# Attention and routed experts on one core: rotary tables kept in device memory, first x tile alone, last output by head pair, new order

## The reference

```python
q = _layernorm(q, q_norm_w, q_norm_b); k = _layernorm(k, k_norm_w, k_norm_b)
q = _rope(q, cos, sin); k = _rope(k, cos, sin)
scores = jnp.einsum('bhqd,bhkd->bhqk', q, k) / math.sqrt(D)
attn = jax.nn.softmax(jnp.where(causal[None, None], scores, -jnp.inf), axis=-1)
out = jnp.einsum('bhqk,bhkd->bhqd', attn, v)
out = out * jax.nn.sigmoid(gate)
return out @ w_o.T
```

## Time and profile before

| | |
|---|---|
| median of 3 runs | 1562.0 us (1560.15 to 1563.43) |
| profiled execution | 1561.02 us |
| its span, from first to last instruction | 1559.2 us |
| TensorE busy | 1508.5 us, 97% |
| TensorE weight loads busy | 1380.0 us, 89% |
| VectorE busy | 1310.9 us, 84% |
| ScalarE busy | 1154.7 us, 74% |
| GpSimd busy | 523.9 us, 34% |
| moved by DMA | 56.65 MB, 36 GB/s in the mean |

### The profile page before, as it was taken

The page is one execution under the profiler, slowest core; times in us unless marked ns, Lnnn a source line. Parts: engine busy times, 40 slices in busy tenths (PEclk is TensorE's granted clock), DMA queues, the critical chain, the costliest instruction groups (busy, mean ns, idle before and its releaser), DMA issues.

```text
span 1559.2 us, 29914 instructions
## 1 busy us (share of the span) xinstructions
PE 1508.5 (97%) x10589; PEld 1380.0 (89%) x10589; DVE 1310.9 (84%) x3011; ACT 1154.7 (74%) x3013; POOL 523.9 (34%) x726
## 2 busy tenths in 40 slices
PE   4999999999899999999999999999999999999998
PEld 3788999999899999999898999999998998899998
DVE  7999888787898888788789888887779988888875
ACT  3777777777778787787778777777777776776775
POOL 5544434320553222121046331221105535343200
PEclk9999999999999999999999999999999999999999
DMA  4400010001111000101211000110111101102000
GB/s 139 142 5 21 21 42 23 21 28 50 45 33 30 32 30 29 32 26 39 66 45 40 25 25 11 47 31 30 28 46 45 33 13 31 30 20 66 16 8 8
DMA packets 46646, 56.65 MB, mean 36 GB/s; under 512 B 4576, under 2 KB 43232, under 8 KB 46304
## 3 DMA queue, kind: packets, MB, share of 16 engines
q1 hardware_dynamic: 43424, 46.34, 9.5%
q0 software_dynamic: 3072, 8.39, 1.7%
HBM read 42.40 MB, written 18.35 MB: 39 GB/s over the span
## 4 chain that ended last, share of the span: by engine, by line
PE 74%; DVE 17%; ACT 5%; issue 2%; POOL 1%; DMA 1%; SPq 0%; DVEq 0%; ACTq 0%; POOLq 0%
PE bank L1286 39%; PE o_bank L1286 19%; PE pt_bank L1361 12%; DVE pT_lo L1219 3%; DVE neg_chunk_max L1205 2%; DVE t_same L1169 2%; DVE bank L1202 2%; PE bank L1339 1%; PE bank L1382 1%; DVE t_same L1165 1%; ACT probs L920 1%; DVE sumsq L1137 1%; DVE t_same L1153 1%; ACT gate L930 1%; ACT pT_hi L939 1%
## 5 line engine op out<-in xcount | busy, mean ns | idle before, releaser
L920 ACT ACTIVATE probs<-bank,neg_max 128x512 f32<-128x512 f32 (+3 forms) x640 | 399.8, 634 | 91.7 <-DVE neg_max L1212 57.6
L1219 DVE TENSOR_TENSOR pT_lo<-pt_bank,pT_hi 128x512 fp32r<-128x512 f32 (+1 forms) x576 | 368.7, 654 | 100.7 <-ACT pT_hi L939 96.8
L939 ACT ACTIVATE pT_hi<-pt_bank 128x512 fp32r<-128x512 f32 (+1 forms) x576 | 325.8, 578 | 131.3 <-PE pt_bank L1361 81.6
L1286 PE MATMUL o_bank<-pT_hi,v_hi 128*128 128x256 f32 x1088 | 333.7, 307 | 2.9 <-DVE pT_lo L1219 1.9
L1361 PE MATMUL pt_bank<-ident_f,probs 128*128 128x128 f32 x2176 | 315.2, 273 | 10.5 <-DVE pT_lo L1219 10.0
L785 POOL TENSOR_TENSOR t_swap<-qk_raw,table_swap 128x256 f32<-128x256 f32 (+1 forms) x256 | 135.4, 560 | 561.9 <-ACT t_same L889 560.9
L1286 PE MATMUL o_bank<-pT_hi,v_lo 128*128 128x256 f32 x1088 | 307.3, 282 | 0.0
L1286 PE MATMUL o_bank<-pT_lo,v_hi 128*128 128x256 f32 x1088 | 306.5, 282 | 0.0
L1205 DVE TENSOR_REDUCE neg_chunk_max<-bank 128x1 f32<-128x512 f32 (+1 forms) x384 | 244.8, 650 | 49.2 <-PE bank L1286 48.1
L1361 PEld LDWEIGHTS pt_bank<-ident_f,probs 128*128 128x128 f32 x2176 | 252.2, 140 | 36.0 <-DVE pT_lo L1219 13.5
L1286 PE MATMUL bank<-kT_hi,qT_hi 128*128 128x512 f32 (+3 forms) x640 | 244.0, 381 | 2.7 <-ACT probs L920 2.3
(11 more groups left out here) (163 smaller groups left out, 2974.6 us busy)
## 6 DMA issues: line engine op xcount, KB each, us to landing
rows<-xs SPq DMA_DIRECT2D x23, 256.0 KB, 2.7
expert_raw<-in_w_fc SPq DMA_DIRECT2D x23, 256.0 KB, 3.0
expert_raw<-in_w_proj SPq DMA_DIRECT2D x23, 256.0 KB, 2.7
yb<-rows SPq DMA_DIRECT2D x23, 256.0 KB, 2.1
xs<-in_x SPq DMA_DIRECT2D x11, 512.0 KB, 4.9
w_raw<-in_w_in SPq DMA_DIRECT2D x7, 640.0 KB, 4.3
angles<-in_cos_sin SPq DMA_DIRECT2D x64, 64.0 KB, 1.9
acc<-in_x SPq DMA_DIRECT2D x4, 512.0 KB, 8.3
```

Of the source, the lines that this page charges most:

```text
L920: act.activation(probs[:, u, h % 2, first:first + width], bank("scores", g, t, h, c)[:, 0:width], ACT.Exp, bias=neg_max[:, u, h % 2:h % 2 ...
L939: act.activation(pT_hi[:, n % PT_RING, 0:width], pt_bank[n % 2][:, 0:width], ACT.Copy)\
L1219: dve.tensor_tensor(pT_lo[:, n % PT_RING, 0:width], pt_bank[n % 2][:, 0:width], pT_hi[:, n % PT_RING, 0:width].bitcast(F32), ALU.subtract) ...
L1286: ins = pe.matmul(out_ap, s, m, start=(start and done == 1), stop=(stop and done == last))
```

## The change

Tables: `tables` stays in group 0 alone. Each set is stored to a new tensor in device memory (`table_store`, 384 KB), and the next `tables` waits until the store has landed. In groups 1 to 3 a load (`table_load`) brings a set back, into the same buffer for odd tiles and into the norm weights' buffer, no longer needed, for even ones. A load waits for all stores and for the rotation of the tile two before. The 48 angle loads of these groups go.

First x tile: the parts of x are 1, 3, 4, 4 and 4 tiles. Tile 0 is turned into one bank in one step.

Last output: for the last tile (3, 15), `og`, `og_hi` and `og_lo` are done by head pair, 256 columns each, and `OUT` is two steps of 6 matmuls into one bank.

Order: all of `BEGIN` and `DUE` are new, `BEGIN` is followed by three shifts for each tile, one for the products and the rotation, one for scores, one for gate and output; some of the planner's costs are new.

```diff
+X_PARTS = ((0, 1), (1, 4), (4, 8), (8, 12), (12, 16))
...
+def shift(g, t, k):
+
+    return BEGIN[2 * G * T + 1 + 3 * (g * T + t) + k]
...
-    for q in range(4):
-        add("sp", ("x_load", q), 0.5, [], 0, 512)
-        if q == 0:
+    for n, (first, last) in enumerate(X_PARTS):
+        add("sp", ("x_load", n), 0.5, [], 0, 128 * (last - first))
+        if n == 0:
...
-        if q == 1:
+        if n == 1:
             add("sp", ("ln_load",), 2.0, [], 0, 260)
...
+            b1, b2 = begin[g, t, 1] + shift(g, t, 2), begin[g, t + 1, 0] + shift(g, t, 2)
+            b0 = begin[g, t, 0] + shift(g, t, 0)
...
+            if g == 0:
+                if t >= 2:
+                    add("sp angles", ("angle_load", g, t), 0.45, [old(t2, "tables")], b0 + DUE["rope"] - 15, 64)
+                table = ("tables", g, t)
+                add("pool rope", table, 4.0, [old(t1, "rope_b"), old(t1, "same"), ("angle_load", g, t), ("ln_tables",),
+                                              ("table_store", t - 1) if t else None], b0 + DUE["rope"])
+                add("sp tables", ("table_store", t), 0.45, [table], 0, 384)
+            else:
+                table = ("table_load", g, t)
+                free = [("tables", 0, T - 1)] if (g, t) == (1, 0) else [old(t2 if n_t != T + 1 else t1, "rope_b")]
+                add("sp tables", table, 0.45, free + [("table_store", T - 1)], b0 + DUE["rope"] - DUE["table"], 384)
...
+            if (g, t) == LAST_TILE:
+                add("pe GT", ("GT", g, t), 0.44, [("gate_scale", g, t), ("o_take", g, t, 0), old(t1, "OUT")],
+                    b2 + DUE["turn_gate"])
+                for p in range(HG // 2):
+                    add("dve out", ("og", g, t, p), 0.33, [("GT", g, t), ("o_take", g, t, p)], b2 + DUE["og"])
+                    add("act og", ("og_hi", g, t, p), 0.3, [("og", g, t, p), old(t1, "OUT")], b2 + DUE["og"])
+                    add("dve og", ("og_lo", g, t, p), 0.33, [("og_hi", g, t, p)], b2 + DUE["og"])
+                add("pe OUT", ("OUT", g, t), 0.72, [("og_lo", g, t, 0), ("wo_lo", g)], b2 + DUE["out"])
+                add("pe OUT", ("OUT_rest",), 0.72, [("og_lo", g, t, 1)], b2 + DUE["out"])
...
+        def rotary(g, t):
+
+            return made_tables if g == 0 or t % 2 else norm_rows
...
+                elif kind == "table_store":
+                    w.wait_ge(tables_done, a[0] + 1)
+                    sp.dma_start(kept_tables[a[0]], made_tables[:]).then_inc(tables_kept, 16)
+                elif kind == "table_load":
+                    g, t = a
+                    n = g * T + t
+                    w.wait_ge(tables_kept, 16 * T)
+
+                    w.wait_ge(tables_done, T)
+                    if n > T:
+
+                        w.wait_ge(rotated_done, n - 1 if n > T + 1 else T)
+                    sp.dma_start(rotary(g, t)[:, 0:3], kept_tables[t]).then_inc(tables_back[t % 2], 16)
...
+                    w.wait_ge(tables_kept, 16 * n)
                     pool.tensor_tensor(halves(table_same[:]), halves(ln_w[:]), cos_t, ALU.mult)
```

More of the change, by code:

```diff
@@ L83, with part_of, turns_of @@
 HANDOVER = {"pe": (0.0, 0.2), "act": (0.28, 0.15), "dve": (0.2, 0.13), "pool": (0.3, 0.16), "sp": (0.2, 0.2)}
-BEGIN = [26.59, 41.38, 29.62, 36.09, 25.65, 50.81, 47.59, 46.92, 64.18, 72.49, 75.23, 89.37, 102.35, 116.24,
[10 rows of a table removed]
[L97 to L102, removed]
+BEGIN = [4.36, 34.3, 51.86, 41.22, 11.3, 27.98, 42.94, 18.5, 56.43, 89.16, 53.77, 79.19, 82.53, 79.26, 113.82,
[22 rows of a table added]
+DUE = {"table": 42.61, "qkv": -42.78, "rope": -12.87, "turn": -307.03, "v_lo": -73.08, "gate": 9.23,
+       "inv": -16.77, "turn_gate": 3.72, "og": 0.09, "out": 10.38, "out_add": 9.58, "scores": -12.51,
+       "max": -8.54, "exp": 27.94, "prob_step": 1.95, "pv": 9.95, "p_hi": -197.39, "p_lo": -1.87, "moe": 348.87,
+       "moe_step": 36.02, "moe_evict": 118.28, "moe_wait_1": 1.57, "moe_wait_2": -3.06, "route": 180.59,
+       "x0": 16.05, "x1": 4.78, "x2": -252.76, "x3": 50.02, "logits": -1.54, "gate_w": -221.0,
+       "scatter": -72.41, "next_w": -70.2, "wo": 702.79, "comb": 135.72, "window": 0.02}
+def part_of(t):
+    return min(n for n, (first, last) in enumerate(X_PARTS) if t < last)
+def turns_of(n):
+    return [(2 * n - 1 + c, c) for c in range(CT)] if n else [(0, None)]
 def chunks_of(t):
@@ L174, in program_steps @@
     add("pool ln", ("ln_tables",), 3.4, [("ln_load",)], 0)
[L175 to L188, removed]
+    when = [0.0, DUE["x0"], DUE["x1"], DUE["x2"], DUE["x3"]]
+    for n, (first, last) in enumerate(X_PARTS):
+        tiles, at = last - first, when[n]
+        add("dve stats", ("stats", n), 0.44 * tiles, [("x_load", n)], at)
+        add("pool x", ("x_rstd", n), 1.4, [("stats", n), ("pool_consts",)], at - 5)
+        add("dve norm", ("norm", n), 0.35 * tiles, [("x_rstd", n)], at)
+        for i, c in turns_of(n):
+            width = tiles * P if c is not None else CT * P
+            add("pe XT", ("XT", i), 0.11 * width / P if n else 0.55, [("norm", n), ("ident_load",)], at + 2)
+            add("act XT", ("xT_hi", i), 0.07 + width / 1200, [("XT", i)], at + 2)
+            add("dve XT", ("xT_lo", i), 0.07 + width / 960, [("xT_hi", i)], at + 2)
+        if n:
+            q = n - 1
+            add("pe L", ("L", q), 1.4, [("xT_lo", 2 * n), ("wr_lo",)], at + DUE["logits"])
+            add("act L", ("logit_copy", q), 0.48, [("L", q), ("LT", q - 1) if q else None], at + DUE["logits"])
+            add("pe L", ("LT", q), 0.25, [("logit_copy", q)], at + DUE["logits"] + 1)
+            add("dve logit", ("route", q), 0.2, [("LT", q)], at + DUE["logits"] + 1)
     for k in range(4, ROUTE_STEPS):
@@ L1010, in _ @@
                 elif kind == "stats":
[L1011 to L1013 removed]
+                    first, last = X_PARTS[a[0]]
+                    w.wait_ge(x_in[a[0]], 16)
+                    for t in range(first, last):
                         dve.bn_stats(x_stats[:, t, :], acc[:, t, :]).then_inc(stats_done, 1)
[L1015 removed]
+                    for t in range(first, last):
                         w.wait_ge(stats_done, t + 1)
@@ L1018, in _ @@
                 elif kind == "norm":
-                    q = a[0]
-                    w.wait_ge(rstd_x_done, 2 * q + 2)
-                    w.wait_ge(means_done, 4 * q + 4)
-                    for t in range(4 * q, 4 * q + 4):
+                    first, last = X_PARTS[a[0]]
+                    w.wait_ge(rstd_x_done, 2 * a[0] + 2)
+                    w.wait_ge(means_done, last)
+                    for t in range(first, last):
                         dve.tensor_scalar(xn[:, t, :], acc[:, t, :], x_mv[:, t, 0:1], x_rstd[:, t:t + 1],
```

158 lines of the change are left out of this document (88 added, 70 removed), and 32 rows, old and new, of the table BEGIN.

## The result

The changed kernel took 1569.8 us (median of 5, 1568.8 to 1571.3), the kernel before beside it 1562.0 (1560.2 to 1563.6). The ratio is 1.0049, interval 1.0034 to 1.0064: slower by 8 us, where 12 faster was forecast. The profiled execution took 1570.0 us, with a span of 1568.2. (Of the four executions behind the 1544.2 one took 3814 us; the other three took 1543.4 to 1544.7, with a median of 1543.7.)

The account below looks back on a forecast made before the run. TensorE was taken as the bound, busy 1508.5 us in a span of 1559.2. Sum: 1561.0 - 3.5 - 0.5 - 4 - 2 - 2 = 1549.0, 1550.0 beside the median; own range 1545 to 1554, whole range 1538 to 1566.

Parts of the forecast that it names:

- The new order: Whole kernel, new begin and due times: 2 us won, ends 11 won and 11 lost.
- not needed by any limit of an engine: Rival: the order does much better, partly from TensorE's 6.7 us idle between 1190 and 1350; 1540 us, chance 0.14.
- signs of being wrong: TensorE losing over 22.3 us from 60 to 1541 us, or VectorE's idle time before 25 us staying over 8.
- Rotary tables: Heads of groups 1 to 3: loaded tables let swaps start early; 3.5 us won, plus 0.5 from VectorE.
- VectorE crossed by GpSimd: Over 1100 us, less GpSimd table work speeds VectorE instructions by perhaps 2 to 6 us; 0.5 us won, ends 0 and 3.
- First x tile: Start of the kernel: a separate first tile wins VectorE idle time before 25 us; 4 us, ends 0 and 9.3.
- the term's first part: Start: norm weights stand behind 512 KB less, 2.9 us at 183 GB/s, of which half was taken.
- Last output: Tail: narrower gate instructions and six of twelve matmuls moved ahead; 2 us won, ends 1.3 and 2.6.
- The stores of the tables: Group 0: a store takes 3.5 us, held by 8.5 us before the next tables; priced at nothing.
- Rival (4): Slower: table loads stand behind waiting instructions on SyncE, 24 us, 1574; chance 0.16 shared with a worse order.
- an order that is worse by 5 or more: Whole kernel: the new order loses 5 us or more; chance 0.16 shared with late table loads on SyncE.

Follow-up runs that it names:

- late chips: Chips of the result and the first, second and fifth sets, where the kernel before took 1560.8 to 1562.0 us; on the others it took 1556.2 or 1556.3.
- r1: The changed kernel itself, unedited, run again on a chip where the kernel before took 1556.2 us: 1544.2 us, ratio 0.9918.
- fourth set: Set of three runs on another chip, the changed kernel unedited among them; the kernel before took 1556.2 us, the changed kernel 1544.2.
- r5: The kernel before with its 32 gathers replaced by GpSimd memsets, where the kernel before took 1560.8 us: 1556.7 us, 0.9973 of before.
- e1: The changed kernel with its 32 gathers replaced by GpSimd memsets of the same rows, same waits and order: 1544.6 us, 0.9893 of the kernel before.
- e10: The kernel before with its 32 gathers replaced by GpSimd memsets, where the kernel before took 1556.3 us: 1555.4 us, 0.9994 of before.
- short rows: The changed kernel gathering rows of 128 bytes instead of 1024: 1544.4 and 1545.2 us on two chips, 1569.1 where the kernel before took 1560.8.
- e4: The changed kernel with 32 more indirect DMAs, scatters into an unused tensor, in four runs of eight: 1585.4 us.
- e2: The changed kernel with its 32 gathers as plain GpSimd loads of the same size at the same places: 1544.9 us.
- e6: The changed kernel with each gather waiting until the one before it in its run of eight has landed: 1608.7 us.
- r6: The changed kernel with a wait ahead of every second gather, two in flight, where the kernel before took 1560.8 us: 1574.6 us.

## Why the prediction was wrong

**The step that failed is "The new order".** It took 2 us won, ends 11 won and 11 lost, and gave as its only reason for a loss that the planner's clock is not the chip's. It has no term for the gathers, so it put their cost at nothing. On the late chips the order lost 21 us on the gathers alone: they cost the changed kernel 25.2 (1569.8 - 1544.6, on two chips) and the kernel before 4.1 (1560.8 - 1556.7, on one chip). The prediction read the due times as a matter of VectorE, never asked where the new order puts the last expert slot, and so never saw that the 32 gathers, begun over 180 us before (1284.6 to 1464.7), would be pressed into 98 (1446.7 to 1544.2). The trace of before had the warning, TensorE's longest wait from 1284 to 1340 us, at 1296.5, behind its run of eight gathers:

```profile
PE pt_bank L1361 <- DVE pT_lo L1219: 2.1, 1, 2.1
```

It lies inside the stretch from 1190 to 1350, whose 6.7 us of idle time I called "not needed by any limit of an engine" and counted as something to win. The loss of 26.3 us of span against r1 is 18.3 of idle time (57.9 against 39.6) and 8.0 more of busy time, as the clock fell after each of the four large gaps (0.97 and 0.88 in the last two stretches, 1.00 in r1).

Both of the prediction's own signs of being wrong came: from 60 to 1541 TensorE loses 27.1 us, over 22.3, and VectorE is idle for 9.1 before 25, over 8. In r1 the first is gone (18.6) and the second is not (8.9).

**Without late updates the sum came out, in part by luck.** 1562.0 to 1550.0 was forecast, 12 us; measured are 12.0 on the fourth set's chip (12.5 by the median of 1543.7), and 12.1 on late chips between the two kernels without gathers (1556.7, 1544.6). The forecast has nearly all of it as idle time of TensorE. Between the traces of these two, r5 and e1, TensorE idles 6.4 us less (47.0, 40.6) and is busy 5.3 us less (1507.6, 1502.3). Most of these 5.3 stand in no term of the forecast, and the start gave less than half of its term. By parts:

- Rotary tables, 3.5 + 0.5 forecast. From 400 to 460 TensorE idles 1.8 us in place of 4.1, and its waits for the rotation fell from 2.7 to 1.2. From 800 to 860 and from 1200 to 1260, in the heads of groups 2 and 3, it idles 0.8 and 0.0 in place of 1.3 and 1.7. That makes 4.5, with what the order did there. The clock of 400 to 460, which the prediction counted too, went from 0.97 to 1.00, but it is 1.00 also in e10 and r5, the kernel before without gathers, so the tables have no part in it. The size is about right, the reason in part wrong. The swaps do start early, but the cycle did not shorten: rotations at 406.76 and 418.15, 11.4 us apart, as before. VectorE, busy 54.4 of the 60 us from 400 to 460, most likely sets the cycle. GpSimd and VectorE of the kernel after, head of group 1:

```profile
402.36 1.99 POOL L874 TENSOR_TENSOR t_swap<-qk_raw,made_tables 128x256 f32<-128x256 f32 x4 [6.32 <-ACT t_same L977]
...
406.76 1.40 DVE L1257 SCALAR_TENSOR_TENSOR t_same<-t_same,rstd,made_tables 128x128 f32<-128x128 f32 x5
...
412.77 1.99 POOL L874 TENSOR_TENSOR t_swap<-qk_raw,norm_rows 128x256 f32<-128x256 f32 x4 [7.15 <-ACT t_same L977]
...
418.15 1.40 DVE L1257 SCALAR_TENSOR_TENSOR t_same<-t_same,rstd,norm_rows 128x128 f32<-128x128 f32 x5
```

- VectorE crossed by GpSimd: the subtraction fell from 768 ns to 689, in the mean of all its tiles, and VectorE's busy time by 6.4 us, while GpSimd's share of the span fell from 34% to 22%. What TensorE had of it can't be read by itself. The row from the kernel after's groups by shape:

```profile
L1328 DVE TENSOR_TENSOR ogT_lo<-oT,ogT_hi 128x512 fp32r<-128x512 f32 x63 | 43.4, 689 | 0.8 <-ACT ogT_hi L1046 0.6
```

- First x tile, 4 forecast: TensorE idles 21.0 us before 60 in place of 22.8, so 1.8. The low half of tile 0's queries came at 33.85, not before 32, and VectorE's idle time before 25 us stayed at 9.1. Before it all stands the wait for the norm weights: GpSimd waited 9.1 us for them, from 4.6 to 13.7, where they had landed at 14.6 before; the term's first part took about 1.5 us for this.
- Last output, 2 forecast: from the start of the last copy out of PSUM to the start of the last addition 3.09 us (1562.58, 1565.67) in place of 5.26. 2.2, right in size, with pieces of 0.42 as forecast. But no six matmuls went ahead by themselves: the twelve still run as one block. It begins 1.32 us after the copy in place of 2.68, since it needs the first half alone, and up to the addition it takes 1.77 in place of 2.58, at the upper clock, where before the clock had fallen. The block in the kernel before and after:

```profile
1554.00:1557.00 3.00, 2.54 (x12) 2.25 (x12) 0.37 (x2) 0.00 (x0) 0.00 (x0) 0.60 0.00 0
1563.00:1566.00 3.00, 1.66 (x12) 1.48 (x12) 1.51 (x4) 0.70 (x2) 0.00 (x0) 1.00 0.00 0
```

  The tail of the kernel after:

```profile
1562.58 0.38 ACT L1036 ACTIVATE oT<-o_bank 128x256 f32<-128x256 f32 x1 [1.92 <-PE o_bank L1379]
...
1563.00 0.42 DVE L1323 TENSOR_TENSOR oT<-bank,oT 128x256 f32<-128x256 f32 x1 [0.23 <-ACT oT L1036]
...
1563.90 0.36 PE L1379 MATMUL bank<-wo_hi,ogT_hi 128*128 128x256 f32 x1 [1.36 <-DVE ogT_lo L1328]
...
1565.67 0.42 DVE L1336 TENSOR_TENSOR acc<-bank,acc 128x256 f32<-128x256 f32 x1 [1.33 <-PE bank L1379]
```

- The order otherwise: from 1190 to 1350 TensorE loses 0.2 us in place of 6.7 (2.7 in r5, the kernel before without gathers), the head of group 3 included; 1.0 less from 60 to 400, 0.8 more from 460 to 1190.
- The stores of the tables, priced at nothing: no wait of GpSimd is put down to one. The estimate of 2.9 us that the prediction worked out for a store from the Trainium skill (DMA: Bandwidth & Descriptors, Anatomy of one DMA) goes by a formula for DMAs that GpSimd issues, and these are SyncE's; no run here shows when a store lands.

**The slower rival was the wrong one.** Rival (4) had table loads late behind SyncE's waits. SyncE did wait, for the rotation that frees a buffer, with others behind it, for up to 29.6 us, but nobody waited for a table: among the waits of GpSimd and VectorE no table load appears. The kernel after, SyncE:

```profile
SPq L776 <- DVE t_same L1257: 507.6, 44, 29.6
SPq L804 <- ACT rows L1079: 340.4, 23, 38.6
```

A rival "an order that is worse by 5 or more" stood in the 0.16 with (4), without a place, a price or a point from which it decides.

Open: why some chips hold updates back. Each chip was seen in one set, so chip and hour can't be told apart. Nor is it shown which part of making an indirect DMA does it, or how long a run may be and how short a pause. One at a time, and two with about 2.5 us of pause, cost nothing by late updates; an unbroken run of eight does. And an instruction without a prompt update in a trace can be a lost record, so the counts above are no count of late updates; the waits in order of time are what shows these. Heads, start and tail were read from stretches, not run alone.

## What to carry to other kernels

When a list scheduler's times change, look first for what it presses together: find the last producer in a chain of transfers and ask what its consumers' issue pattern becomes, since a run of indirect DMAs is not priced as eight times one. Spread indirect DMAs, with the consumer's place moved back to match, for a consumer in a fixed list stands for the whole latency. Waits between them alone made the changed kernel slower on both sorts of chip (1573.9, 1574.6, and 1608.7 one at a time). Run the unchanged kernel beside every experiment and compare its time from one set of runs to the next: had I not, short rows would stand here as the cause.

## What the runs showed of the hardware

- While GpSimd issues a run of eight indirect DMAs of 128 rows without a pause (1.25 us apart, two or three in flight), semaphore updates of TensorE reach ScalarE and VectorE up to about 4.5 us late on some chips. It costs 4 us of time for each such run in the middle of the kernel (e4: 16 us for four) and 6 at its end, where the clock falls too (25 us for four). Plain loads of the same size from GpSimd, 0.56 us apart, do no such harm (e2), nor do indirect DMAs one at a time (e6) or in pairs with about 2.5 us of pause (r6).
- It was there beside the result and in three of the five sets of runs, each on its own chip, and not in the other two. One program took 1569.8 us on one chip and 1544.2 on another, 1.7% apart.
- An indirect DMA of 128 KB alone takes 3.45 us from issue to issue, 0.95 of it on GpSimd (e6).
